# Attention: probabilities and values turned by DMA instead of TensorE, and contexts two places behind the scores

## What is computed

```
y    = einsum('bct,bcd->bdt', x, weights[itok])          # a 64 x 64 matrix for each sample
qkv  = y @ W_qkv + b_qkv                                  # 4096 positions x 3072, fp32
p    = softmax(q k^T / sqrt(32))                          # 64 samples x 32 heads, 64 x 64 each
x    = x + (p @ v) @ W_o + b_o
x    = x + ffn(lora_experts(x))                           # the second half, not touched
```

## Time and profile before

| | before |
|---|---|
| median of 3 executions | 2261.29 us |
| the profiled execution | 2260.01 us |
| its span, first to last instruction | 2258.3 us |
| mean granted TensorE clock | 0.986 of 2.4 GHz |
| TensorE matmul busy | 2172.7 us, 96% |
| VectorE busy | 1437.8 us, 64% |
| GpSimd busy | 1383.6 us, 61% |
| ScalarE busy | 732.3 us, 32% |

### The profile page before, as it was taken

How to read it: one execution, slowest core, us unless ns; L and a number is a source line. 1 busy time by engine, 2 the same in 40 slices (tenths; PEclk the granted TensorE clock), 3 DMA queues, 4 the chain that set the end, 5 groups by cost and what they waited for, 6 DMA issues and landing times.

```text
span 2258.3 us, 46591 instructions
## 1 busy us (share of the span) xinstructions
PE 2172.7 (96%) x18816; PEld 1774.4 (79%) x18848; DVE 1437.8 (64%) x2399; ACT 732.3 (32%) x1182; POOL 1383.6 (61%) x1134
## 2 busy tenths in 40 slices
PE   6999999999999999999999899999999999999997
PEld 5888887888877888878888778888777777777875
DVE  5345564455464454554554786656689888888887
ACT  4222243222242222332222432222443444443442
POOL 5888778877778877698777650000355455555554
PEclk9999999999999999999999899999999999999998
DMA  4111222211132112212111644557644344444343
GB/s 146 54 64 62 67 85 71 76 53 62 62 100 67 65 53 65 75 60 72 56 59 50 223 137 143 183 190 187 178 101 109 94 102 112 109 104 104 93 100 93
DMA packets 220972, 219.35 MB, mean 97 GB/s; under 512 B 83586, under 2 KB 152322, under 8 KB 220290
## 3 DMA queue, kind: packets, MB, share of 16 engines
q1 hardware_dynamic: 217938, 213.65, 31.7%
q0 software_dynamic: 2864, 3.28, 0.9%
HBM read 152.92 MB, written 50.33 MB: 90 GB/s over the span
## 4 chain that ended last, share of the span: by engine, by line
PE 83%; DVE 8%; issue 3%; SPq 2%; ACT 2%; DMA 1%; POOL 1%; DVEq 0%; ACTq 0%; POOLq 0%
PE acc L699 34%; PE acc L1615 15%; PE acc L1095 6%; PE att L1095 6%; PE att L1642 5%; PE att L730 3%; PE att L1585 3%; PE acc L1651 2%; PE att L739 2%; PE att L754 2%; DVE prob L539 2%; PE acc L1624 2%; PE acc L713 1%; DVE total L535 1%; SPq L265 1%
## 5 line engine op out<-in xcount | busy, mean ns | idle before, releaser
L699 PE MATMUL acc<-y_hi,w_slot_hi 128*128 128x512 f32 x1344 | 542.0, 403 | 25.7 <-issue 7.3
L699 PE MATMUL acc<-y_lo,w_slot_hi 128*128 128x512 f32 x1344 | 528.1, 393 | 0.0
L699 PE MATMUL acc<-y_hi,w_slot_lo 128*128 128x512 f32 x1344 | 527.8, 393 | 0.0
L345 POOL TENSOR_TENSOR w_slot_lo<-w_raw,w_slot_hi 128x512 fp32r<-128x512 f32 x329 | 424.6, 1290 | 26.3
L699 PEld LDWEIGHTS acc<-y_hi,w_slot_hi 128*128 128x128 f32 x1344 | 254.6, 189 | 85.8 <-issue 32.4
L343 POOL CAST w_slot_hi<-w_raw 128x512 fp32r<-128x512 f32 x329 | 218.0, 663 | 156.1 <-PE acc L699 131.6
L699 PEld LDWEIGHTS acc<-y_hi,w_slot_lo 128*128 128x128 f32 x1344 | 254.8, 190 | 54.9
L699 PEld LDWEIGHTS acc<-y_lo,w_slot_hi 128*128 128x128 f32 x1344 | 255.2, 190 | 48.2
L348 POOL TENSOR_TENSOR w_raw<-w_raw 128x512 f32<-128x512 f32 x188 | 259.3, 1379 | 29.8 <-DMA w_raw<-wu 26.0
L546 DVE COPY cx<-att 128x512 f32<-128x512 f32 x63 | 43.6, 692 | 306.0 <-PE att L754 276.9
L556 DVE TENSOR_TENSOR unit<-acc,unit 128x512 f32<-128x512 f32 x144 | 98.8, 687 | 176.1 <-PE acc L699 171.9
(11 more groups left out here) (179 smaller groups left out, 3931.4 us busy)
## 6 DMA issues: line engine op xcount, KB each, us to landing
w_raw<-wu SPq DMA_DIRECT2D x192, 256.0 KB, 3.1
c_raw<-context_T SPq DMA_DIRECT2D x16, 1024.0 KB, 6.7
f_x_all<-x_T SPq DMA_DIRECT2D x32, 512.0 KB, 4.9
f_xr_all<-x_T SPq DMA_DIRECT2D x32, 512.0 KB, 6.1
context_T<-cx SPq DMA_DIRECT2D x63, 256.0 KB, 3.5
out<-f_raw SPq DMA_DIRECT2D x31, 512.0 KB, 3.4
x_raw<-x SPq DMA_DIRECT2D x27, 512.0 KB, 4.5
xa<-xT SPq DMA_DIRECT2D x12, 1024.0 KB, 7.5
```

The lines of the kernel that those rows point to most:

```text
L345: pool.tensor_tensor(w_lo[:, k], raw, w_hi[:, k].bitcast(F32), ALU.subtract).then_inc(w_set, 1)
L699: ins = pe.matmul(bank, w[:, k, c, :], v[:, k, c, :], start=(k in (0, 1, 5) and c == 0 and i == 0), stop=(c == C // 2 - 1 and i == 2), ski ...
```

## The change

- **Probabilities.** For the iterations 0 to 60 TensorE turns nothing. Each half `prob[:, p]` (128x512 fp32) is seen as 16-bit words. ScalarE copies the low words and the high words into two planes, `pw[:, p]` (128 x 2 x 512 of uint16), waits for its own copy, and issues from its own queue a DMA transpose of 128x1024 16-bit elements into `pv[:, p]`. Later it joins the planes into `prob_T[:, p]` with one more copy. The last three iterations are turned on TensorE as before.
- **Values.** The same for all 64 value tiles, through `vw` and `vv` to `v_s`.
- **Places.** Scores stand at 0, 5, 10 and 15. The exponential is in the same slot as the scores (before, in the next). VectorE normalises half 0 one slot and half 1 two slots after the scores. ScalarE sends half 0 out two and half 1 three slots after, and takes both back six slots after. The context of iteration n stands with the scores of n + 2, ten slots after its own scores. Values go out at the places 0, 7, 9, 14 and come back at 3, 9, 13, 18 (in the last duo at 0, 2, 4, 6 and 2, 4, 6 and in the tail).
- **Buffers.** The planes lie over `x_raw0` to `x_raw2`. So the first three tiles of x for the next block are loaded only in the last unit (k = 4 and 5), behind waits for the turns. After a block end y is staged in `uo[0]` instead of `uo[1]`.
- **Tail.** The context of iteration 60 and half of the normalising of 61 move behind the last unit, and the first load for the output stage (`xa`) moves behind it too.

The diff, cut to its core:

```diff
@@ scalar @@
-        def turn_v(duo, q):
+        def prob_out(n, p):
+            x_done(n)
+            act.wait_ge(prob_set, n * 2 + p + 1)
+            act.activation(pw[:, p], words(prob[:, p]), ACT.Copy).then_inc(pw_set, 1)
+            act.wait_ge(pw_set, n * 2 + p + 1)
+            act.dma_start_transpose(pv[:, p], pw[:, p].rearrange("p h n -> p (h n)"))\
+                .then_inc(p_in[p], 16)
+
+        def prob_back(n, p):
+            if n and p == 0:
+                act.wait_ge(c_mm, n)
+            act.wait_ge(p_in[p], 16 * (n + 1))
+            act.activation(words(prob_T[:, p]), pv[:, p].rearrange("p (h j) n -> p h (j n)", h=2), ACT.Copy)\
+                .then_inc(pT_set, 1)
+
+        def v_out(n):
...
+            act.activation(vw[:], words(uo[1][:, 2 * g + half]), ACT.Copy).then_inc(vw_set, 1)
+            act.wait_ge(vw_set, n + 1)
+            act.dma_start_transpose(vv[:], vw[:].rearrange("p h n -> p (h n)"))\
+                .then_inc(v_in, 16)
+
+        def v_back(n):
...
+            act.wait_ge(v_in, 16 * (n + 1))
+            act.activation(v_s[:, 4 * half:4 * half + 4, g * P:(g + 1) * P].bitcast(U16)
+                           .rearrange("p j (f h) -> p h j f", h=2),
+                           vv[:].rearrange("p (h j) f -> p h j f", h=2), ACT.Copy).then_inc(v_set, 1)
@@ scalar, the walk over the slots @@
-                if scored(*last) is not None:
-                    att_exp(scored(*last))
-                if turned(U, k) is not None:
-                    att_pt(turned(U, k))
-                duo, turns = values(U, k)
-                for q in turns:
-                    turn_v(duo, q)
+                if behind(U, k, 6) is not None:
+                    prob_back(behind(U, k, 6), 0)
+                    prob_back(behind(U, k, 6), 1)
+                if values_back(U, k) is not None:
+                    v_back(values_back(U, k))
+                if values_out(U, k) is not None:
+                    v_out(values_out(U, k))
+                if scored(U, k) is not None:
+                    att_exp(scored(U, k))
+                for p in range(2):
+                    if (behind(U, k, 2 + p) or 0) < TURNED and behind(U, k, 2 + p) is not None:
+                        prob_out(behind(U, k, 2 + p), p)
@@ tensor, the walk over the slots @@
-                if mixed(U, k) is not None:
-                    att_ctx(mixed(U, k))
-                if turned(U, k) is not None:
-                    att_turn(turned(U, k))
-                duo, turns = values(U, k)
-                for q in turns:
-                    turn_v(duo, q)
-                if scored(U, k) is not None:
-                    att_scores(scored(U, k))
+                n = scored(U, k)
+                if n is not None:
+                    att_scores(n)
+                    if n > 1:
+                        att_ctx(n - 2)
@@ sync @@
+                if U % UNITS == UNITS - 1 and r + 1 < BLOCKS:
+                    for i in {4: (0,), 5: (1, 2)}.get(k, ()):
+                        load_x((r + 1) * PAIRS + i)
```

More of the change, by code:

```diff
@@ L164, in place, with behind, values_out, values_back @@
         return divmod(q, 3 * SLOTS) if q >= 0 else (-1, -1)
+    PLACES = (0, 5, 10, 15)
     def scored(U, k):
         duo, at = place(U, k)
-        return 4 * duo + (0, 4, 10, 15).index(at) if at in (0, 4, 10, 15) else None
-    def turned(U, k):
+        return 4 * duo + PLACES.index(at) if at in PLACES else None
+    def behind(U, k, steps):
+        q = SLOTS * U + k - steps
+        return scored(*divmod(q, SLOTS)) if q >= 0 else None
+    def values_out(U, k):
         duo, at = place(U, k)
-        return 4 * duo + (3, 9, 14, 19).index(at) if at in (3, 9, 14, 19) else None
-    def mixed(U, k):
+        steps = (0, 2, 4, 6) if duo == DUOS - 1 else (0, 7, 9, 14)
+        return 4 * duo + steps.index(at) if at in steps else None
+    def values_back(U, k):
         duo, at = place(U, k)
[L178 to L185, removed]
+        steps = (2, 4, 6) if duo == DUOS - 1 else (3, 9, 13, 18)
+        return 4 * duo + steps.index(at) if at in steps else None
+    def words(ap):
+        return ap.bitcast(U16).rearrange("p (n h) -> p h n", h=2)
+    TURNED = ITERS - 3
     HIGHS, LOWS_DVE, LOWS_POOL = (0, 5, 1, 2, 3, 4, 6), (0, 5, 3), (1, 2, 4, 6)
@@ L228, in x_tile, with stage @@
         return uo[2 * (i // 2)][:, 2 * (i % 2):2 * (i % 2) + 2].rearrange("p a n -> p (a n)")
+    def stage(r):
+        return uo[0] if r else uo[1]
     def y_bank(p):
@@ L249, in load_x @@
             tile = r * PAIRS + t // 2 + PAIR * (t % 2)
-            if i >= PAIRS + 3:
+            last = 16 * r - 4
+            if r and t >= 3:
                 sp.wait_ge(y_mm, i - 2)
-            elif i >= PAIRS:
-                sp.wait_ge(y_mm, i - PAIRS + 1)
-            arrived = x0_in[i // 2 - 1] if 3 <= i < PAIRS else x_in[(i - PAIRS) % 3 if i >= PAIRS else i]
+            elif r:
+                sp.wait_ge(y_mm, PAIRS * r)
+                if t == 0:
+                    sp.wait_ge(v_set, last + 1)
+                elif t == 1:
+                    sp.wait_ge(p_in[0], 16 * (last + 1))
+                    sp.wait_ge(p_in[1], 16 * (last + 1))
+                else:
+                    sp.wait_ge(pT_set, 2 * (last + 1))
+            arrived = x0_in[i // 2 - 1] if 3 <= i < PAIRS else x_in[t % 3]
             sp.dma_start(x_tile(i), x[tile]).then_inc(arrived, 16)
@@ L300, in sync @@
             if U % UNITS == 0 and r + 1 < BLOCKS:
-                for i in range(3):
-                    load_x((r + 1) * PAIRS + i)
                 load_wc(r + 1, range(PAIRS))
             for k in range(SLOTS):
-                if mixed(*before(U, k)) is not None:
-                    store(mixed(*before(U, k)))
+                n = scored(*before(U, k))
+                if n and n > 1:
+                    store(n - 2)
                 if U == ALL - 1:
                     after.sync_early(sp, k)
+                if U % UNITS == UNITS - 1 and r + 1 < BLOCKS:
+                    for i in {4: (0,), 5: (1, 2)}.get(k, ()):
+                        load_x((r + 1) * PAIRS + i)
                 if U + 2 < ALL:
@@ L320, in sync @@
         after.sync_early(sp, SLOTS)
-        for n in range(LAST - 2, ITERS):
+        for n in range(LAST - 3, ITERS):
             store(n)
@@ L455, in refill_y @@
             act.wait_ge(y_mm, 2 * n + 1)
-            act.activation(uo[1][:, p % 2], bank[:, Y11], ACT.Identity).then_inc(r11_set, 1)
+            act.activation(stage(r)[:, p % 2], bank[:, Y11], ACT.Identity).then_inc(r11_set, 1)
             if r and p == 0:
@@ L701, in product @@
             ins.then_inc(prod_mm, 1)
-        def turn_v(duo, q):
-            g, half = TURN_V[q]
-            V = 3 * duo + 1
-            if q == 2:
-                pe.wait_ge(act_out, 4 * V + 4)
-            else:
-                pe.wait_ge(dve_out, 3 * V + (3, 1, 0, 2)[q])
-            if 4 * duo + q > 1:
-                pe.wait_ge(v_set, 4 * duo + q - 1)
-            for j in range(HALF // P):
-                ins = pe.transpose(acc[:, 2 + q % 2, j * P:(j + 1) * P], uo[1][:, 2 * g + half, j * P:(j + 1) * P], ident[:])
-            ins.then_inc(vt_mm, 1)
         def att_scores(n):
@@ L744, in att_ctx @@
             g, half = it // 2, it % 2
-            pe.wait_ge(pt_set, n * 2 + 2)
+            if n < TURNED:
+                pe.wait_ge(pT_set, n * 2 + 2)
+            else:
+                pe.wait_ge(pt_set, (n - TURNED) * 2 + 2)
             pe.wait_ge(v_set, 4 * duo + it + 1)
```

91 lines of the change are left out of this document (54 added, 37 removed).

## The result

The changed kernel takes 2232.83 us (median of 4, 2227.16 to 2237.58). The kernel before takes 2261.70 us beside it (2256.12 to 2263.11). The ratio is 0.988, 95% interval 0.985 to 0.991: it is faster, by 29 us. The forecast was 63.

The account below looks back on a forecast made before the run. TensorE's list of matmuls was taken to bound the attention stage. Removed turns and waits, 94.7 us, less 21 and 3 for stalls and 7.7 in the last unit, gave 63: 2260 - 63 = 2197 us, range 2166 to 2236.

Parts of the forecast that it names:

- the last unit: End of the attention stage: ScalarE's list of 31.3 us starts the tail about 5 us later; 7.7 us back.
- the block ends: Late x tiles in SyncE's queue cost nothing, covered by 6 us; without cover up to 4 us per block end.
- the stalls at places 0 and 7: TensorE waits for ScalarE's PSUM emptying, 0.7 and 0.6 to 0.7 us; 21 us, plus 3 at block starts.
- The waits of 11.4 us: TensorE's waits for normalised probabilities (4.8 us) and VectorE's PSUM emptying (6.6 us) should go with the turns.
- ScalarE's copies: Each plane copy of 1024 16-bit elements per partition takes 1.05 us on ScalarE, bounds 0.60 and 2.1 us.
- Issue and landing: A DMA transpose holds ScalarE's queue 1.24 us, lands 3.0 us after issue; DMA engines under a half busy.
- GpSimd: a step that failed: GpSimd's work of 57.9 us a duo leaves 8 of 66 us, and it runs a unit ahead of TensorE.
- ScalarE somewhat heavier: Rival, chance 0.22: a copy at 1.4 us or an issue near 2 us gives 2223 to 2228 us.
- a bound ScalarE: Rival, chance 0.10: copies at 2.1 us make ScalarE's duo 78.2 us, so the kernel takes 2365 us.
- a slow landing: Rival, chance 0.03: turns landing in 10.5 us hold ScalarE 3.5 us four times a duo, 2370 us.
- a hidden turn: Rival, chance 0.02: the turns were hidden anyway, so the time stays 2260 us.
- the one without stalls: Rival, chance 0.10: issues don't hold ScalarE's queue and both tight places fit, 2168 us.

Follow-up runs that it names:

- the quartered turns: Kernel before, with one 128x128 transpose instead of four in most probability and value turns on TensorE, outputs wrong: 2209.61 us, ratio 0.979.
- v_places: Changed kernel with value turns moved to places with room in 12 of 16 duos: 2232.97 us, ratio 0.986 to the kernel before.
- five edits: Changed kernel with x tiles loaded earlier, output-stage loads held back, GpSimd's splits reordered, joins written densely, value turns moved; all together 2184.00 us, ratio 0.965.
- control: The changed kernel run again without edits: 2230.35 us, ratio 0.987 to the kernel before.

## Why the prediction was wrong

The range of 2166 to 2236 us takes in the result, at its upper end. The central value erred by 36 us, and less than half of the saving forecast came. What bounds the kernel and what is removed were right; the costs set against it were not. By size: the last unit, put at 7.7 us, cost 26; the block ends, put at nothing, cost 12.7 us of waits for x in one execution and 5.0 in the other, and would have taken whatever was gained within the blocks, because GpSimd had no slack; the stalls at places 0 and 7 cost 30 for 24.

- *What bounds the kernel, what is removed.* Right. TensorE's list was the bound and the removal is worth its rows: the quartered turns gave 51 us, and up to the last unit TensorE's busy time fell by 79.3 us where 80.6 of turns were removed. The waits of 11.4 us were half right: those for L556 went (6.6 to 0.2), and the waits for probabilities left their ten places, but the one behind the last unit grew by 5.2 us.
- *ScalarE's copies.* The parting copy was right (1.05). The joining copy measured 1.37, a third above the term of the sum. The reason given against it, that the rows of 1024 elements agree whatever type is written, failed: none of these rows wrote with a stride. The Trainium skill's note on cachelines ("SBUF — State Buffer", "Door 1: The DMA port swizzle"), by which such a stride is free, agrees with the strided read at 1.05 us, and not with the strided write.
- *Issue and landing.* 1.25 us and 3.3 us by the medians, as taken from the earlier trace rows; a turn in an attention stage held up nobody. The share of the DMA engines was 0.53, where "under a half" stood.
- *Places 0 and 7.* The two places are the ones named, at 1.07 and mostly 0.89 us where 0.7 stood. The size was 29.8 us for 24. How much of that is the heavier join isn't shown: with joins at 1.18 the waits were 2.7 us less, in one execution, and the two executions of the changed kernel differ by 3.5. ScalarE's busy 41.7 of 75 us is the 40 forecast.
- *GpSimd: a step that failed.* "19.3 us a unit ... still leaves it 8, and it runs a whole unit ahead." The busy time is right, and busy time was the wrong measure. The period of the loop is 22.3 us, because R22's reload of about 4 us stands in it. 66.9 us against a duo of 67.4 leaves 0.5, not 8. Nor did it run a unit ahead: an engine a whole unit ahead waits for TensorE's slot, and it did so for 0.5 us. The sign was in the trace of before: 16 waits for weights (26.0 us) by an engine that was supposed to have a unit to spare. In the changed kernel this costs TensorE only 2.0 us directly; it comes to bear through SyncE's queue.
- *SyncE's queue and the block ends: the second.* "I cost this at nothing; ... without it each of the three block ends would lose up to 4 us." The queue has a load ahead of tiles 1 and 2 that waits for GpSimd. It cost 12.7 us in the one execution, 5.0 in another, and it took the 22 us that `v_places` saved: up to 12.3 at one block end.
- *The last unit: the third, and the largest.* "7.7 us back"; it was about 26 (the 23.5 of the table and the 2.7 not gained), in both executions. Left out was that the turns share the DMA engines with 6 MB of loads: an issue that held ScalarE 6.00 us, and a landing for which it stood 7.4 us. With these loads held back the stretch is 8.6 us shorter, so this is about half of the missing 18.5. The other half is that the list "about 5 us later" was too short: without the collision the tail's scores still come 10.2 us late, behind heavier joins and a landing. And "the rest of the tail is ... unchanged" isn't so: at a granted clock of 0.57 it took 24.1 us from its scores to the output stage, before 17.1 at 0.68. The sum rests on the DMA share in the middle of the attention stage (0.19), not on that of this place, where before it was 0.48 in the unit's first 20 us and 0.80 in the next 25 already.
- *The rivals.* "ScalarE somewhat heavier" gives 2223 to 2228, nearest to the result, and its copy of 1.4 us is what the joins measured. But only half the copies are so, the issue near 2 us that it also allowed wasn't seen (1.25), and as the cause it isn't borne out: with the dense write alone, in one execution, nothing was gained. That its time comes nearest is luck. The rivals of a bound ScalarE, a slow landing and a hidden turn are out; so is the one without stalls.

What stays open: how the 18 us before the last unit divide between the loop and ScalarE's stalls in any one execution, since each waits for the other; and how much of the tail's loss is the lower clock and how much its own order, as no run parts the two.

## What to carry over

Measure the slack of a helper engine by what it waits for, not by its busy share: a load into a buffer that the helper itself has just freed is part of its period, and an engine that already waits for such loads has little room. When work is moved to another queue, look at each place along it for the load that waits for somebody else, and at the DMA share in the fullest stretch, not the typical one. An edit that shows nothing alone can be worth much once the limit beside it is loosened, so try them together before dropping one: here five edits of which the best gave 14 us alone, by medians, gave 49 together.

## What the hardware showed

- ScalarE copies 1024 16-bit words per partition in 1.05 us when it reads every second word and writes densely, and in 1.37 us when it writes every second word. With a strided read in another order and a dense write it took 1.18.
- A 128x1024 transpose of two bytes issued on ScalarE's queue holds that engine 1.25 us. Beside loads of 1 MB each one issue held it 6.00 us (4.67 to 6.03 in the five other profiled runs that leave these loads there, 1.25 at that place with the loads held back), and a landing took up to 12.4 us (14.3 in `control`, 8.2 with the loads held back), where the usual one takes 3.0 to 3.3.
- The value turns land later than the probability turns, 4.5 us against 3.3 by the medians, at the same size. No run tells why.
